# Fourteen expert units started beside the last batches' routing, in a fused attention and mixture-of-experts kernel

## Chip, cores and metric

One core of one Trainium2 chip. The metric is the device time of one execution in microseconds (us). The engines are TensorE (PE; PEld are its weight loads), VectorE (DVE), ScalarE (ACT), GpSimd (POOL) and SyncE (SP), which mostly issues DMAs.

## The reference, cut to what matters

```python
S, D, heads of 64, E, R, K = 512, 512, 8, 8, 128, 2        # x, ctx_1024: (8, 512, 512) float32
# attention of x over ctx_1024, per batch and head
q, k, v = layernorm(x) @ Wq, ctx @ Wk, ctx @ Wv
x = x + tanh(g_xattn[0]) * (softmax(q k^T / 8) v @ Wo + bo)
# mixture of experts, on all 4096 tokens
z = layernorm(x)
topv, topi = top_k(z @ gate_w, 2);  w = softmax(topv)
u, v = z @ Wu[e], z @ Wv[e]                                 # e: each token's two experts
x = x + tanh(g_ffn[0]) * sum over the two of  w * (silu(u) * v) @ Wo[e]
```

The router gives each of the 4096 tokens two of eight experts, so the eight lists hold 8192 entries in all, of sizes that depend on the data.

## The kernel before, in words

**Attention.** Batches b = 0 to 7 have four steps j each, so g = 4b + j runs from 0 to 31. A step handles two heads: their scores, the softmax and its product with V, and beside it the projections of q and k for two heads to come, and work on the next batch's tokens. Numbers are carried as a float16 high part and a low part, with three products (PASSES) for one. An exponential needs the row maximum first: `row_max_scores` makes an approximate score block per head h and tile t on PE (L1275), 8 a step, `row_max` reduces it on DVE (L873), and `max_transpose` (L1280) turns the result. PE's order is written out by hand in `step`.

**Second norm and routing.** A step g of batch b also finishes a 128-token tile n = g - 4 of the batch before: transposes of the heads' output into oT (`transposes`, L1242), `out_project` (12 products of 128x512, L1233), `x2_rows` on DVE, store of the new x to the output. Then come `factors2`, `normalise2` and `row_lo`, which make the normed row's two halves, `turn` (a DMA transpose) and `logits`. After four tiles `best_two`, `ranks`, `take_ranks` and `places` give each token its place in the two lists, and `scatter` on POOL writes its row (2064 bytes) there with 8 indirect DMAs for a batch (L576). The ring of rows has 6 slots. All the G products of attention and routing take turns in two PSUM banks, in the order that `bank_uses` lists.

**Tail.** Batch 7's tiles have no later step, so a loop over g = 32 to 37 does them alone. It also makes the logits and places of batch 6. `unit_table` on DVE then lists the units: a unit is a window of UR = 256 rows of one expert's list, and there are UNITS = 32 + 7 = 39 of them, of which the ones beyond the real blocks repeat rows of the last list with weight 0.

**Units.** SP loads a unit's 256 rows (516 KB, 6 slots ahead), PE turns them (L1449), multiplies by the expert's weights (L1457, L1468), ACT scales (L830), and POOL adds the two tiles of results onto the output with two indirect accumulating DMAs (L662). Two units may name the same token. So `unit(s)` always waits until unit s - 2's adds have landed, and where the expert changes or two windows of one list overlap also for those of unit s - 1. That is what `need` says:

```python
if 0 < s < 3:
    pool.wait_ge(added[(s - 1) % 2], 2 * 16)
if s >= 3:
    before = pool.value_load(need[0:1, s:s + 1], min_val=2 * 16, max_val=32 * UNITS)
    pool.wait_ge(added[(s - 1) % 2], before)
```

Within a list the last block goes first, then the others from the start. ACT writes results into a ring of 4, so it waits for the adds of unit s - 4.

## Time and profile before

| | us |
|---|---|
| median of 3 runs | 1108.74 |
| their range | 1103.36 to 1109.86 |
| the profiled execution | 1095.86 |
| its span, first to last instruction | 1094.1 |

The span is what the trace shows; 1.76 us lie around it. The profiled execution is one run, and faster than the three timed ones. A view's start times are counted from the span's start, L numbers are lines of the kernel before, and in brackets behind a row stands how long the engine was idle before it and what ended that.

### The profile page before, as it was taken

The numbers are of one execution on the slowest core, as the hardware profiler recorded it, in microseconds if no ns is written. First come the engines' busy times: TensorE is split into PE (matmuls) and PEld (weight loads), VectorE is DVE, ScalarE is ACT, GpSimd is POOL, SyncE is SP. The second block draws the span as 40 slices with busy tenths as digits, with TensorE's granted clock in tenths as the row PEclk, the third lists the DMA queues.
The fourth block names the chain that finished last, engine by engine and source line by source line (L and its number), as shares of the span: only waits on it lengthen the run. The fifth ranks groups of instructions, "written<-read, shape, count | busy, mean of one in ns | idle before, by whom it ended". The sixth has DMA issues, their size and how long they took to land.

```text
span 1094.1 us, 22759 instructions
## 1 busy us (share of the span) xinstructions
PE 902.0 (82%) x8210; PEld 546.8 (50%) x8210; DVE 677.7 (62%) x1595; ACT 570.5 (52%) x1022; POOL 536.3 (49%) x645
## 2 busy tenths in 40 slices
PE   4888878998899899899899989886650899799890
PEld 2344435555455455455555545443320777677660
DVE  5687757777777767767777776586234454344440
ACT  4366646566556656556655656456210465555450
POOL 6122324253465366447546543645563146666564
PEclk9999989999999999999999999998665899999995
DMA  8555773422362264254336228334343588999996
GB/s 274 154 161 158 236 244 78 141 73 74 97 199 71 65 199 112 60 177 112 76 88 208 67 63 266 95 93 146 97 142 105 151 195 170 181 195 194 185 159 81
DMA packets 125325, 154.26 MB, mean 141 GB/s; under 512 B 48288, under 2 KB 81056, under 8 KB 124832
## 3 DMA queue, kind: packets, MB, share of 16 engines
q1 hardware_dynamic: 108352, 115.40, 36.0%
q0 software_dynamic: 16864, 37.40, 17.8%
q8 instruction: 69, 1.13, 0.4%
q14 instruction: 40, 0.33, 0.1%
HBM read 62.83 MB, written 56.30 MB: 109 GB/s over the span
## 4 chain that ended last, share of the span: by engine, by line
PE 51%; DVE 12%; DMA 11%; issue 9%; ACT 7%; POOL 6%; SPq 2%; POOLq 1%; ACTq 0%; DVEq 0%
PE G L1233 26%; DMA out_dram<-V,Ph 7%; PE MX L1275 4%; PE ST L1290 3%; PE ST L1289 3%; PE MX L1457 3%; PE G L1242 3%; POOL out_dram L662 2%; PE PV L1302 2%; PE PV L1304 2%; PE PV L1306 2%; DVE tiles L863 2%; DVE mx L873 2%; POOL expert_rows L576 2%; PE G L1449 1%
## 5 line engine op out<-in xcount | busy, mean ns | idle before, releaser
L619 POOL TENSOR_TENSOR Pl<-P,Ph 128x512 f16<-128x512 f32 x128 | 150.6, 1184 | 223.5 <-ACT Ph L697 223.0
L694 ACT ACTIVATE P<-ST 128x512 f32<-128x512 f32 x256 | 153.3, 599 | 203.3 <-PE ST L1290 194.4
L873 DVE TENSOR_REDUCE mx<-MX 128x1 f32<-128x512 f32 x256 | 168.1, 684 | 26.4 <-PE MX L1275 26.4
L697 ACT ACTIVATE Ph<-ST 128x512 f16<-128x512 f32 x256 | 154.6, 604 | 0.4
L662 POOL DMA_INDIRECT out_dram<-V,Ph x78 | 122.5, 1571 | 48.1 <-ACT V L830 28.4
L1457 PE MATMUL MX<-heads,tiles 128*128 128x256 f16 x936 | 119.8, 280 | 16.5 <-DVE heads L1187 16.3
L1302 PE MATMUL PV<-V,Ph 128*128 128x65 f16 x1024 | 114.2, 196 | 23.0 <-issue 23.0
L1302 PEld LDWEIGHTS PV<-V,Ph 128*128 128x128 f16 x1024 | 97.9, 98 | 43.8 <-issue 26.2
L1304 PE MATMUL PV<-V,Ph 128*128 128x64 f16 x1024 | 114.5, 197 | 0.0
L1306 PE MATMUL PV<-V,Pl 128*128 128x65 f16 x1024 | 114.1, 195 | 0.0
L1457 PEld LDWEIGHTS MX<-heads,tiles 128*128 x936 | 91.5, 100 | 38.6 <-issue 21.3
L1304 PEld LDWEIGHTS PV<-V,Ph 128*128 128x128 f16 x1024 | 97.4, 99 | 18.6 <-issue 1.1
L1289 PE MATMUL ST<-heads 128*128 128x512 f16 x256 | 98.6, 385 | 6.7 <-DMA heads<-mrow 3.8
L1290 PE MATMUL ST<-heads 128*128 128x512 f16 x256 | 98.8, 386 | 0.0
L1306 PEld LDWEIGHTS PV<-V,Pl 128*128 128x128 f16 x1024 | 97.8, 101 | 0.0
L911 DVE TENSOR_TENSOR Pl<-P,Ph 128x512 f16<-128x512 f32 x128 | 95.9, 751 | 2.5 <-ACT Ph L697 2.5
L1275 PE MATMUL MX<-heads 128*128 128x512 f16 x256 | 89.2, 384 | 9.4 <-DVE mx L873 9.2
L1233 PE MATMUL G<-tiles,wq_hi 128*128 128x512 f16 x256 | 79.0, 391 | 12.9 <-DVE tiles L863 12.9
L1233 PE MATMUL G<-wv_hi,tiles 128*128 128x512 f16 x256 | 81.7, 379 | 0.0
L563 POOL TENSOR_TENSOR second_norm<-second_norm,tgbo 128x512 f32<-128x512 f32 x32 | 42.5, 1328 | 74.1 <-DMA second_norm<-in_x_dram 73.8
L1233 PE MATMUL G<-tiles,wk_hi 128*128 128x512 f16 x256 | 76.2, 379 | 0.2 <-DVE k_lo L863 0.2
L918 DVE SCALAR_TENSOR_TENSOR second_norm<-G,gate,second_norm 128x512 f32<-128x512 f32 x32 | 24.0, 750 | 84.0 <-PE G L1233 78.1
(206 smaller groups left out, 1917.6 us busy)
## 6 DMA issues: line engine op xcount, KB each, us to landing
heads<-expert_rows SPq DMA_DIRECT2D x39, 516.0 KB, 5.5
tiles<-in_x_dram SPq DMA_DIRECT2D x32, 256.0 KB, 4.8
tiles<-in_ctx_dram SPq DMA_DIRECT2D x32, 256.0 KB, 5.2
second_norm<-in_x_dram SPq DMA_DIRECT2D x32, 256.0 KB, 3.2
out_dram<-second_norm SPq DMA_DIRECT2D x32, 256.0 KB, 2.4
heads<-q_hi SPq DMA_DIRECT2D x124, 64.0 KB, 2.0
heads<-k_hi SPq DMA_DIRECT2D x124, 64.0 KB, 2.0
expert_rows<-second_norm SPq DMA_DIRECT2D x2, 2064.0 KB, 11.0
```

What stands on the lines that cost most here:

```text
L619: nc.gpsimd.tensor_tensor(Pl[:, hh, c, :], P32[:, c, :], Ph[:, hh, c, :], ALU.subtract).then_inc(pl_pool, 1)
L662: nc.gpsimd.indirect_dma_start(out_rows, bass.IndirectOffsetOnAxis(ids[:, s, k:k + 1], 0), y_sb[:, s % YR, k, :], None, compute_op=ALU.add) \
L694: nc.scalar.activation(P32[:, c, :], ST[:, c % 2, :], ACT.Exp, scale=0.125 / SC2).then_inc(p_ready, 1)
L697: nc.scalar.activation(Ph[:, hh, c, :], ST[:, c % 2, :], ACT.Exp, scale=0.125 / SC2).then_inc(ph_ready, 1)
L873: nc.vector.tensor_reduce(out=mx[:, k // TT, k % TT:k % TT + 1], in_=MX[:, (k + odd) % 2, :], axis=AXX, op=ALU.max).then_inc(mx_taken, 1)
L1233: last = nc.tensor.matmul(out_, a, m, start=(n == 0), stop=(n == len(parts) - 1))
L1275: nc.tensor.matmul(MX[:, (k + g) % 2, :], Q1[:, s, h, t * P:(t + 1) * P], K1[:, s, h, :], start=True, stop=True).then_inc(mx_filled, 1)
L1290: nc.tensor.matmul(ST[:, c % 2, :], K2[:, j, hh, cols], Q2[:, j, hh, :], start=False, stop=True).then_inc(st_filled, 1)
L1302: nc.tensor.matmul(out_[:, 0:HD + 1], Ph[:, hh, c, cols], V[:, r, c, h, 0:HD + 1], start=(c == 0), stop=False)
L1304: nc.tensor.matmul(out_[:, 0:HD], Ph[:, hh, c, cols], V[:, r, c, h, HD + 1:], start=False, stop=False)
L1306: last = nc.tensor.matmul(out_[:, 0:HD + 1], Pl[:, hh, c, cols], V[:, r, c, h, 0:HD + 1], start=False, stop=(c == TT - 1))
L1457: last = nc.tensor.matmul(dst, w, uT[:, s % 2, a, c * UR:(c + 1) * UR], start=k == 0, stop=k == len(parts) - 1)
```

## The change

1. **Early units.** After step 30, when batches 0 to 5 have their places, `early_table` (DVE, some 32 small instructions) picks EARLY = 14 units among blocks that are full already. It takes level by level, one block from the end of each list's full blocks, then a second one of the first lists that have it, and lists them by expert. `unit_table` is cut into `unit_experts`, `unit_windows` and `unit_needs` for the LATE = 25 other units, which skip the blocks taken.
2. **Interleaving.** The tail loop is gone. Its work stands in gaps v = 0 to 10 (GAPS = 11) of the unit loop on every engine, by `tail_uses`, `between`, `ahead_of` and `late_in`. The G banks are then shared by units and tail: each side waits for the other's evacuations. SP requests the rows of the first six units when the scores are done and batches 0 to 5 are scattered, and from unit 14 on waits for the late table and all scatters.
3. **Buffers.** Batch 7's residuals are loaded at once into the idle O buffer (`x2_of`), its rows go into the wq and wk buffers (`row_of`), and the early table lies in xn.
4. **Output waits.** Adds of units 0 to 13 wait only for the stores of batches 0 to 5; unit 14 for all stores and for unit 13's adds. In the late list a change of expert needs no wait when one window lies wholly below, the other wholly above `cut`, each list's length after batch 4.
5. **Row maxima.** `row_max_scores` contracts over 64 rows instead of 128: head 0 of a pair from partitions 0 to 63, head 1 from 64 to 127, each into its own MX bank, and the two follow one another on PE.

Cut to its core; `late=True` in PE's `between` is the place behind the v products:

```diff
+def tail_uses(v, first, late):
+    if late:
+        return [("out", first + v)] if v <= 3 else [("ranks", first // 4)] if v == 8 else []
+    names = [("oT", first + v)] if v <= 3 else []
+    if v in (0, 2):
+        names.append(("logits", first - 2 + v // 2))
+    if v == 4:
+        names.append(("ranks", first // 4 - 1))
+    if 4 <= v <= 7:
+        names.append(("logits", first + v - 4))
+    return names
...
+            def between(v):
+                n = TILES - TT + v
+                if v == 0:
+                    turn(n - 1)
+                if 1 <= v <= 4:
+                    store_x2(n - 1)
+                if 2 <= v <= 5:
+                    turn(n - 2)
+            load_last_residuals()
+            sp.wait_ge(early_ready, 3)
+            sp.wait_ge(st_filled, STEPS * 8)
+            for r in range(2):
+                for h in range(2):
+                    sp.wait_ge(scattered[r][h], EARLY_BATCHES // 2 * 2 * K * 16)
+            for s in range(XG):
+                unit_rows(s)
             for s in range(UNITS):
-                unit_rows(s)
+                if s < GAPS:
+                    between(s)
+                if s + XG == EARLY:
+                    sp.wait_ge(table_ready, 2)
+                    sp.wait_ge(outsider_st, E * K * 16)
+                    for r in range(2):
+                        for h in range(2):
+                            sp.wait_ge(scattered[r][h], B // 2 * 2 * K * 16)
+                if s + XG < UNITS:
+                    unit_rows(s + XG)
             for r in range(2):
...
+            def between(v):
+                n = TILES - TT + v
+                if v == 0:
+                    factors2(n - 1)
+                    add_bias(n)
+                    row_lo(n - 1)
+                    for t in range(1, TT):
+                        add_bias(n + t)
+                if 1 <= v <= 4:
+                    factors2(n - 1)
+                if v in (5, 9):
+                    scatter(B - 2 + v // 9, 0)
+                    scatter(B - 2 + v // 9, 1)
+            def unit_add(s):
                 pool.wait_ge(ids_ready, s + 1)
-                if 0 < s < 3:
-                    pool.wait_ge(added[(s - 1) % 2], 2 * 16)
-                if s >= 3:
-                    before = pool.value_load(need[0:1, s:s + 1], min_val=2 * 16, max_val=32 * UNITS)
-                    pool.wait_ge(added[(s - 1) % 2], before)
+                if s in (0, EARLY):
+                    for r in range(2):
+                        pool.wait_ge(x2_st[r], (EARLY_BATCHES * TT if s == 0 else TILES) // 2 * 16)
+                if s and (s < 3 or s == EARLY):
+                    pool.wait_ge(added[(s - 1) % 2], ((s - 1) // 2 + 1) * 2 * 16)
+                elif s:
+                    wanted = pool.value_load(listed(e_need, l_need, s)[0:1], min_val=2 * 16, max_val=32 * UNITS)
+                    pool.wait_ge(added[(s - 1) % 2], wanted)
...
-            for s in range(UNITS):
-                unit(s)
+            pool.wait_ge(early_ready, 3)
+            for v in range(UNITS + 2):
+                if v < GAPS:
+                    between(v)
+                if v == EARLY + 1:
+                    pool.wait_ge(table_ready, 3)
+                if v >= 2:
+                    unit_add(v - 2)
+                if 1 <= v <= 4:
+                    row_lo(TILES - TT + v - 1)
...
+                nc.vector.tensor_tensor(above, limit, cut_u, ALU.is_ge)
+                nc.vector.tensor_tensor(flag[:, ahead], off[:, here], off[:, ahead], ALU.subtract)
+                link(nc.vector.scalar_tensor_tensor(out=below, in0=limit, scalar=float(UR), in1=cut_u,
+                                                    op0=ALU.add, op1=ALU.is_le))
+                nc.vector.tensor_tensor(done[:, ahead], below[:, ahead], above[:, here], ALU.mult)
+                link(nc.vector.tensor_tensor(blocks[:, ahead], above[:, ahead], below[:, here], ALU.mult))
+                nc.vector.tensor_tensor(first_[:, ahead], l_ue[:, here], l_ue[:, ahead], ALU.not_equal)
+                link(nc.vector.tensor_tensor(done[:, ahead], done[:, ahead], blocks[:, ahead], ALU.max))
+                nc.vector.tensor_scalar(blocks[:, ahead], flag[:, ahead], float(-UR), None, ALU.is_gt)
+                link(nc.vector.tensor_tensor(first_[:, ahead], first_[:, ahead], done[:, ahead], ALU.is_gt))
+                link(nc.vector.scalar_tensor_tensor(out=flag[:, ahead], in0=flag[:, ahead], scalar=float(UR),
+                                                    in1=blocks[:, ahead], op0=ALU.is_lt, op1=ALU.mult))
+                link(nc.vector.tensor_tensor(flag[:, ahead], flag[:, ahead], first_[:, ahead], ALU.max))
+                nc.vector.scalar_tensor_tensor(out=l_need[:, here], in0=flag[:, ahead], scalar=32.0,
+                                               in1=C["need"][:, EARLY:UNITS - 1],
+                                               op0=ALU.mult, op1=ALU.add).then_inc(table_ready, 1)
...
+                link(nc.vector.tensor_scalar(below_all, level_sum, float(EARLY), None, ALU.is_le))
+                link(nc.vector.tensor_reduce(level, below_all, AXX, ALU.add))
+                nc.vector.tensor_tensor(e_cum[:, 0, :], full, level.to_broadcast([P, E]), ALU.is_gt)
+                link(nc.vector.tensor_tensor(used, full, level.to_broadcast([P, E]), ALU.min))
+                link(nc.vector.tensor_reduce(spare_sum, used, AXX, ALU.add))
+                link(nc.vector.tensor_scalar(spare_sum, spare_sum, -1.0, float(EARLY), ALU.mult, ALU.add))
...
             def row_max_scores(g, k):
                 s, turn = slot_and_use(g)
-                h, t = k // TT, k % TT
+                t, h = divmod(k, 2)
+                rows_ = slice(h * HD, (h + 1) * HD)
                 if k == 0:
                     pe.wait_ge(qk_dma[s], turn * QK_DMAS * 16)
                 if k == 1:
                     since(pe, mrow_ready, g)
                 else:
                     since(pe, mx_taken, g * (2 * TT) + k - (1 if k > 1 else 0))
-                nc.tensor.matmul(MX[:, (k + g) % 2, :], Q1[:, s, h, t * P:(t + 1) * P], K1[:, s, h, :],
+                nc.tensor.matmul(MX[:, h, :], Q1[rows_, s, h, t * P:(t + 1) * P], K1[rows_, s, h, :],
                                  start=True, stop=True).then_inc(mx_filled, 1)
...
                     n = "qk"[k // 2]
                     scores(b, j, k)
-                    maxima(2 * k)
+                    maxima(2 * k, 2 * k + 1)
                     if proj and k % 2 == 0:
                         dst = bank((n, g))
                         if j == 2 and k == 0:
                             pe.wait_ge(evacuated, use[n, g])
                         product(dst, parts[n], 0, 6)
-                    maxima(2 * k + 1)
...
-            pe.wait_ge(table_ready, 1)
-            pe.wait_ge(evacuated, len(uses))
+                return pe.value_load(listed(e_expert, l_expert, s)[0:1], min_val=0, max_val=E - 1)
+            pe.wait_ge(early_ready, 1)
             unit_transposes(0)
             for n in "uvo":
                 pe.wait_ge(fw_back[n], 16)
             e = expert_of(0)
             for s in range(UNITS):
+                if s < GAPS:
+                    between(s, False)
                 pe.wait_ge(t_hi, s + 1)
                 pe.wait_ge(t_lo, s + 1)
                 since(pe, a_done, s)
...
                     unit_transposes(s + 1)
                 since(pe, s_done, s)
                 up("v", Vp, e, s, v_filled)
+                if s < GAPS:
+                    between(s, True)
                 if s:
                     down(s - 1, e_before)
                 e_before = e
+                if s == EARLY - 1:
+                    pe.wait_ge(table_ready, 1)
                 if s < UNITS - 1:
                     e = expert_of(s + 1)
             down(UNITS - 1, e_before)
```

## Rows read from the trace of the kernel before

**Rows 1.** The page: busy time of each engine
```profile
PE 902.0 (82%) x8210; PEld 546.8 (50%) x8210; DVE 677.7 (62%) x1595; ACT 570.5 (52%) x1022; POOL 536.3 (49%) x645
```

**Rows 2.** Stretches: busy (count) of PE, PEld, DVE, ACT, POOL; PEclk, DMA share, GB/s
```profile
260.00:660.00 400.00, 365.75 (x3500) 208.65 (x3498) 295.85 (x665) 238.64 (x443) 215.68 (x275) 0.99 0.41 112
780.00:785.00 5.00, 3.50 (x10) 1.17 (x9) 0.69 (x1) 2.00 (x3) 1.15 (x1) 0.50 0.04 8
...
865.00:965.00 100.00, 93.11 (x872) 73.24 (x870) 48.41 (x170) 54.63 (x93) 57.36 (x50) 0.98 0.87 182
```

**Rows 3.** Timeline where attention ends and where units began: start, length, engine, line
```profile
772.76 0.96 POOL L576 DMA_INDIRECT expert_rows<-second_norm,pos_staged  x1 [0.30 <-issue]
...
842.08 0.96 POOL L576 DMA_INDIRECT expert_rows<-second_norm,pos_staged  x1 [0.30 <-issue]
...
846.15 2.65 SPq L522 DMA_DIRECT2D heads<-expert_rows  x3
...
849.86 1.44 PE L1449 MATMUL G<-identity,heads 128*128 128x128 f16 x12 [20.16 <-DMA heads<-expert_rows]
```

**Rows 4.** POOL's timeline: adds of results (L662), two a unit
```profile
865.16 1.61 POOL L662 DMA_INDIRECT out_dram<-V,Ph  x1 [12.17 <-ACT V L830]
...
893.19 1.56 POOL L662 DMA_INDIRECT out_dram<-V,Ph  x1 [3.07 <-ACT V L830]
895.05 1.57 POOL L662 DMA_INDIRECT out_dram<-V,Ph  x1 [0.30 <-issue]
900.77 0.19 POOL L543 TENSOR_TENSOR junk<-ones 128x1 f32<-128x1 f32 x1 [4.15 <-DMA out_dram<-V,Ph]
901.46 1.56 POOL L662 DMA_INDIRECT out_dram<-V,Ph  x1 [0.50 <-issue]
...
905.27 1.56 POOL L662 DMA_INDIRECT out_dram<-V,Ph  x1 [0.16 <-POOL junk L543]
...
1082.02 1.56 POOL L662 DMA_INDIRECT out_dram<-V,Ph  x1 [0.44 <-issue]
```

**Rows 5.** PE's timeline: row transposes of two units in a row
```profile
889.23 1.06 PE L1449 MATMUL G<-identity,heads 128*128 128x128 f16 x16
...
894.04 1.06 PE L1449 MATMUL G<-identity,heads 128*128 128x128 f16 x16
```

**Rows 6.** The table of waits in the unit stage: us, times, longest
```profile
POOL junk L543 <- DMA out_dram<-V,Ph: 43.7, 8, 6.8
```

**Rows 7.** PE's timeline in attention: two row-maximum products in a row
```profile
395.20 0.59 PE L1275 MATMUL MX<-heads 128*128 128x512 f16 x2
```

**Rows 8.** PE's timeline: transposes to score product, without and with the small transpose
```profile
338.44 0.63 PE L1242 MATMUL G<-identity,tiles 128*128 128x128 f32 x4 [0.77 <-DVE oT_lo L863]
338.90 0.38 PE L1289 MATMUL ST<-heads 128*128 128x512 f16 x1
...
403.63 0.63 PE L1242 MATMUL G<-identity,O 128*128 128x128 f32 x4 [0.30 <-DVE k_lo L863]
404.10 0.27 PE L1280 MATMUL MX<-identity,mneg 128*8 128x128 f32 x1
404.20 0.38 PE L1289 MATMUL ST<-heads 128*128 128x512 f16 x1
```

**Rows 9.** Timelines of POOL (residual, scatters) and of DVE (unit table)
```profile
763.01 1.26 POOL L563 TENSOR_TENSOR second_norm<-second_norm,tgbo 128x512 f32<-128x512 f32 x1 [5.38 <-DMA second_norm<-in_x_dram]
...
803.02 0.19 POOL L543 TENSOR_TENSOR junk<-ones 128x1 f32<-128x1 f32 x1
...
812.47 0.96 POOL L576 DMA_INDIRECT expert_rows<-second_norm,pos_staged  x1 [0.30 <-issue]
...
831.85 0.16 DVE L1011 TENSOR_TENSOR nt<-base,list_starts 128x8 f32<-128x8 f32 x1
...
841.57 0.20 DVE L1055 SCALAR_TENSOR_TENSOR Ph<-Ph,adds_before 128x38 uint32<-128x38 f32 x1
```

**Rows 10.** PE's waits in attention: us, times, longest
```profile
PE G L1242 <- DVE oT_lo L863: 15.0, 9, 2.4
```

More of the change, by code:

```diff
@@ new lines, in layer @@
+        l_ids = take(K * LATE).bitcast(U32).rearrange("p (u k) -> p u k", k=K)
+        valid = take(K * LATE).rearrange("p (u k) -> p u k", k=K)
+        spare_n = xn[:].rearrange("p k d -> p (k d)")
+        at = Count()
+        take = lambda n: spare_n[:, at.take(n):at.value]
+        e_ue, e_expert, e_off, e_need = (take(EARLY) if k == 0 else take(EARLY).bitcast(U32) for k in range(4))
+        e_uw = take(4 * EARLY).rearrange("p (k u) -> p k u", k=4)
+        levels = take(EB * E).rearrange("p (l e) -> p l e", l=EB)
@@ new lines, in layer, with listed @@
+        level_sum, below_all, level, spare_sum = take(EB), take(EB), take(1), take(1)
+        e_ids = take(K * EARLY).bitcast(U32).rearrange("p (u k) -> p u k", k=K)
+        e_cmp = take(E * BE).rearrange("p (e b) -> p e b", e=E)
+        e_ucmp, e_ucmp2 = (take(EARLY * E).rearrange("p (u e) -> p u e", e=E) for _ in range(2))
+        e_cum = take(4 * E).rearrange("p (k e) -> p k e", k=4)
+        full, low, cut = take(E), take(E), take(E)
+        used = take(E)
+        def listed(early, late, s):
+            return early[:, s:s + 1] if s < EARLY else late[:, s - EARLY:s - EARLY + 1]
@@ L1004, in outsiders, with running_sum, unit_experts @@
                 nc.vector.tensor_tensor(out_pos[:], before, spare_place, ALU.add).then_inc(outsider_ready, 1)
-            def unit_table():
-                spread_e = lambda z: z.unsqueeze(1).to_broadcast([P, UNITS, E])
-                spread_u = lambda z: z.unsqueeze(2).to_broadcast([P, UNITS, E])
-                before, block_, limit, off, over, blocks, flag = (uw[:, k, :] for k in range(7))
+            def running_sum(z):
+                for k, d in enumerate((1, 2, 4)):
+                    nc.vector.tensor_copy(z[:, k + 1, 0:d], z[:, k, 0:d])
+                    link(nc.vector.tensor_tensor(z[:, k + 1, d:E], z[:, k, d:E], z[:, k, 0:E - d], ALU.add))
+            spread_e = lambda z: z.unsqueeze(1).to_broadcast([P, LATE, E])
+            spread_u = lambda z: z.unsqueeze(2).to_broadcast([P, LATE, E])
+            first_, j_, limit, off, start_, blocks, flag, done, cut_u, below, above, over = (uw[:, k, :] for k in range(12))
+            def unit_experts():
+                number = C["unit_no"][:, 0:LATE]
+                nc.vector.tensor_tensor(low, full, used, ALU.subtract)
                 link(nc.vector.tensor_tensor(nt[:, 0, :], base[:], C["start"][:], ALU.subtract))
@@ L1433, in _, with between, ahead_of_turn @@
             pe.wait_ge(o_ready, B * HB)
-            for g in range(STEPS, STEPS + 6):
-                if g < STEPS + 4:
-                    transposes(("oT", g - 4), O[(B - 1) % 2][:, g - STEPS, :])
-                    out_project(g - 4)
-                logits(g - 6)
-                if g % 4 == 1:
-                    ranks(g // 4 - 2)
+            def between(v, late):
+                for name in tail_uses(v, TILES - TT, late):
+                    what, n = name
+                    if what == "out":
+                        out_project(n)
+                    elif what == "oT":
+                        transposes(name, O[(B - 1) % 2][:, v, :])
+                    elif what == "logits":
+                        logits(n)
+                    else:
+                        ranks(n)
+            def ahead_of_turn(s):
+                names = [n for v in range(min(s, GAPS)) for late in (False, True)
+                         for n in tail_uses(v, TILES - TT, late) if not (late and v == s - 1)]
+                return 1 + max(use[n] for n in names) if names else use["oT", TILES - TT]
             def unit_transposes(s):
                 r = s % XG
+                units_turned.take()
                 pe.wait_ge(rows_ld[r], (s // XG + 1) * 16)
+                pe.wait_ge(evacuated, ahead_of_turn(s))
                 for a, taken in ((0, t_hi), (1, t_lo)):
```

321 lines of the change are left out of this document (189 added, 132 removed).

## The prediction

> **What bounds the kernel now.** I read the page's busy shares first, then a table by stage, then the waits and the timelines. TensorE (PE) is busy for 82% of the span [rows 1], but the stages differ [rows 2]. In attention (260 to 660 us) PE is busy 91% of the time at a clock share of 0.99, with DVE at 74%. From 780 us, when the last head is done, to 850 us, PE almost stops: that is the routing of the last batches, a chain of small steps through every engine. Then come 39 units. Their first 256 rows are requested at 846.15, PE turns them at 849.86, and the first add of a result is issued at 865.16 [rows 3, 4]. The last unit's add is issued at 1082.02 [rows 4], 12.1 us before the span ends at 1094.1.
>
> In the unit stage the queue that sets the pace is GpSimd's (POOL's). A PE unit takes 4.81 us when nothing holds it (889.23 to 894.04) [rows 5], so 38 intervals would be 183 us. The adds take 216.9. The reader should see two kinds of interval in their timeline. A free one is 3.81 us (901.46 to 905.27): two issues and a small POOL instruction. A held one waits until the adds of the unit before have landed: 895.05 + 1.57 ends the issue, 4.15 us of wait follow, and the next add starts at 901.46, 8.27 us after 893.19 [rows 4]. So a held interval is 4.12 us plus its wait. The table of waits has 8 such waits of 43.7 us together, 5.46 on average and 6.8 at the longest [rows 6]: 9.6 us on average, 10.9 at most.
>
> I worked out the routing from the reference's inputs. The eight lists have 1147, 971, 688, 1113, 1074, 929, 1219 and 1051 tokens, 36 blocks. Units 1 and 2 always wait. Each of the 7 changes of expert holds, and so does the first of the 3 spare units: 10 held intervals, which is two more than the 8 of the table (the first two end with ACT). Counted alike the held ones take 10 x 9.6 = 96 us, and the 28 others (216.9 - 96)/28 = 4.3 on average.
>
> **The change, part by part.**
>
> (a) The units' start moves. The last scatter of batch 5 is issued at 772.76 [rows 3]. Before, the last scatter of all, at 842.08, was followed by the request for rows 4.07 us later; the same step gives 776.8, and with 3.7 us to landing 780.5, more with six requests together: 782.5. Before, first transposes to first add took 15.3 us [rows 3, 4]. Now PE also has, ahead of unit 0's down product, two blocks of oT transposes (0.63 each), two output projections of 12 matmuls at a pitch of 0.21 us, 2.5 us each [rows 7, 8], and their evacuations, much of it at the half clock (0.50 at 780 to 785, 1.2 GHz) [rows 2]: about +10 us. First add: 782.5 + 25.5 = 808 instead of 865.2, **57 us earlier**.
>
> (b) The adds wait more often. Early units go one level at a time, so experts change often. Batches 0 to 5 give 3, 2, 1, 3, 3, 2, 3, 3 full blocks; 14 units are 2, 2, 1, 2, 2, 2, 2, 1 of them. Held are units 1, 2, 4, 5, 7, 9, 11, 13, and 14 by a fixed wait. Of the 22 real late units the rule on token ranges releases only some: a list's last low block beside the next list's end. But lists 0, 3, 4, 6 and 7 have a further block above the early ones, and that one comes last, so ten transitions stay held, plus the first spare unit. Together **20 held and 18 free intervals instead of 10 and 28**. Nothing else on POOL hides them, as the same queue issues every add.
>
> (c) The last batches' routing goes beside units 0 to 10. PE then needs about 10 us a unit in the first two intervals: 4.8 + 2.5 + 0.6, and the shared G banks make each piece wait for the evacuation of the last. On POOL, ahead of adds 3 and 7, stand eight scatters, 803.02 to 813.43, 10.4 us [rows 9]; with the issues of the add before them (3.4) and a start of 0.5 an interval is 14.3, and the landing of the add before is hidden under them. The residual additions, the row splits and the factors lie in the waits of held adds. The unit table, 831.85 to 841.57 [rows 9] on an idle PE before, is cut into three pieces beside units 8 to 10; its some 60 instructions cost nothing as long as POOL is behind, and up to 10 us if it is not. Unit 14's rows wait for scatter 7; PE reaches them at about the same time: 0 to 3 us, I take 0.
>
> (d) The sum. Which price has a held interval? The DMA engines were 0.87 busy from 865 to 965 us [rows 2]; the same bytes, spread over some 50 us more, load them less. Between 8.3 and 9.6 I take 8.9. A free one is POOL's own pace more often now, between 3.81 and 4.3: 3.9. Two intervals at 10, two at 14.3, seventeen held at 8.9 = 151.3, seventeen free at 3.9 = 66.3: 266.2 us against 216.9, **49.3 us more**. First add 57 earlier, chain 49 longer: **8 us gained**. With 8.3 and 3.8 it is 20; with 9.6 and 4.3 it is 11 us lost.
>
> (e) The early table, some 32 small DVE instructions, stands between steps 30 and 31: 7 us by the pace of the old table (39 in 9.9). Step 31 was held by POOL, which waited 5.38 us for a residual until 763.01 [rows 9], so most is covered: 0 to 7, I take **2 lost**.
>
> (f) The row-maximum products now use 64 rows each, the two heads of a pair in the two halves of the array, side by side, in fixed banks. Before, two in a row are recorded with 0.59 us and one product of that width with 0.38 [rows 7, 8], a pitch of 0.21 us each. If the halves run together a pair saves 0.15 to 0.2; 4 pairs in 31 steps are 124 pairs, 19 to 25 us of PE. Does it reach the end? PE is 91% busy in attention, its waits there are on DVE and ACT hand-overs, such as 15.0 us on oT_lo [rows 10], and these would grow; I count 0.65: **12 us gained**. If they run one after the other it is 0. The odd products also move ahead of half a projection, which gives DVE its maxima earlier; but PE's largest wait is another one; taken as 0.
>
> What does a change of the array's shape cost? The trace has one: the transpose of the maxima uses 8 columns, on a 32-column tile. With it, four transposes to the next score product take 0.57 us (403.63 to 404.20); without it 0.46 (338.44 to 338.90) [rows 8]. The difference, 0.11, is the small transpose itself, so two changes of shape cost next to nothing. The Trainium skill, "TensorEngine Tiling (Array Packing)", Key Properties, says that tiles can execute matmuls in parallel, but that changing the tiling mode drains TensorE. By that drain the sum would turn: that is rival 2. The row is of a change in columns, not in rows, so it doesn't settle it.
>
> In all: 1095.86 - 8 + 2 - 12 = 1078, by the profiled execution, which had 1.76 us around its span. It was 12.9 us faster than the median shown, 1108.74; scaled, the forecast is **1091 us**, 1.6% faster. A measurement of this kernel can hardly tell under 1% from no change.
>
> **Rivals.**
>
> 1. The adds' queue eats it all (slower). The long waits for landing stay at 9.6 us and free intervals at 4.3: (d) loses 11, (e) 2, and (f) brings nothing because DVE and ACT hold PE: 1109, scaled 1122. It decides from a held interval of 9.35 us, where at 3.9 for the free ones the 57 us are used up. For it: the number of held intervals doubles. Against it: the load falls.
>
> 2. The halves drain the array. A 512-column product is recorded for 0.38 us at a pitch of 0.21 [rows 7, 8], so a drain could show 0.16 at each side of a pair: 0.33 lost, 0.15 won, 22 us over 124 pairs, of which I count 18. With the 8 and the 2: 1108, scaled 1121. For it only the page; against it the trace's one change of shape [rows 8].
>
> 3. The halves don't overlap and cost nothing, everything else as forecast: 1090, scaled 1103, within 1%.
>
> 4. Better than forecast: landings fall to 4.15 us of wait and PE keeps all it wins: 1095.86 - 20 + 1 - 20 = 1057, scaled 1070.
>
> **How the numbers follow.** Forecast (the case of 1082 to 1098) 0.38, rival 4 (1062 to 1082) 0.18, rival 3 (1098 to 1110) 0.20, rival 1 0.12, rival 2 0.12. Faster by over 1% (under 1097.7) is the first two, with a little of rival 3: 0.58. Slower by over 1% (over 1119.8) is half of the last two and a tail: 0.14. The rest, 0.28, is within 1%. The range of 8 in 10 reaches from 1066 to 1120.
>
> **What would show it.** (a) The first add at 805 to 812. (b) 20 intervals of 8 to 10 us, nine of them up to add 14. (c) Two gaps of about 14 us with the scatters in them. (d) Last add at about 1062 to 1068, if attention is shorter by 10 to 12 us. (f) Pairs of 64-row products that start less than 0.1 us apart, and a product after them no later than 0.3 us from the first; and attention's last head 8 to 15 us earlier. Wrong it would be if held intervals cost over 9.4, if the pairs are 0.4 us or longer, or if the first four units go at over 12 us each because of the G banks and the half clock; each us there is 4 on the first adds.

## The result, and the profile after

The kernel before: 1106.21 us (median of 7 runs, 1100.50 to 1109.86). The changed kernel: 1113.46 us (7 runs). The ratio is 1.0085, 95% interval 1.0051 to 1.0119. It is taken from the changed kernel's six runs that were not slow by chance (the seventh took 1121.42); the quotient of the two medians shown is 1.0066. The changed kernel is slower by a little under 1%, where 1.6% faster had been forecast. The time lies in the range of 1066 to 1120, but above 1110, where only rivals 1 and 2 stood, with 0.12 each. The profiled execution of after took 1118.5 us, its span 1116.8.

The busy line of its page answers to [rows 1]:

```profile
PE 913.6 (82%) x8210; PEld 533.8 (48%) x8210; DVE 686.0 (61%) x1648; ACT 570.2 (51%) x1022; POOL 537.8 (48%) x645
```

The stretches of after, as in [rows 2]:

```profile
260.00:660.00 400.00, 361.72 (x3446) 196.08 (x3445) 295.51 (x659) 235.02 (x437) 216.54 (x273) 0.99 0.41 111
...
800.00:850.00 50.00, 40.86 (x342) 28.35 (x341) 24.22 (x87) 21.15 (x35) 21.57 (x32) 0.89 0.50 115
850.00:900.00 50.00, 33.58 (x290) 24.47 (x288) 24.72 (x121) 15.32 (x26) 32.36 (x35) 0.84 0.80 198
```

PE is busy for the same share as before. The idle stretch of [rows 2] at 780 us is gone, but at 850 to 900 us, where units were to run at full pace, PE is idle a third of the time. The hand-over, from the timelines of SP, PE and POOL in after, answers to [rows 3, 4]; the last row is the last unit's first add:

```profile
787.48 2.91 SPq L566 DMA_DIRECT2D heads<-expert_rows  x3
...
791.66 1.65 PE L1644 MATMUL G<-identity,heads 128*128 128x128 f16 x14 [4.68 <-DMA heads<-expert_rows]
...
817.00 1.67 POOL L734 DMA_INDIRECT out_dram<-V,xn  x1 [0.41 <-issue]
...
1104.35 1.56 POOL L734 DMA_INDIRECT out_dram<-V,Ph  x1 [0.58 <-issue]
```

The adds began at 817.0 instead of 865.2 and ended at 1104.4 instead of 1082.0. Their chain took 287.4 us instead of 216.9. The table of waits of after in the unit stage, us, times and longest, answers to [rows 6]:

```profile
POOL junk L612 <- DMA out_dram<-V,Ph: 55.8, 11, 7.2
...
POOL junk L612 <- DMA out_dram<-V,xn: 32.5, 6, 6.5
```

17 waits of 88 us stand where 8 of 44 stood, 5.2 us each on average instead of 5.5. To see where the time went, I cut the span at three landmarks that both traces have: DVE's last copy of row maxima in attention (745.34 before, 752.06 after), the first add, and the last. The last column is a second trace of the changed kernel (e8, below):

| stretch | before | forecast | after | after again |
|---|---|---|---|---|
| start to the last row maxima | 745.3 | -12 | +6.7 | -0.4 |
| from there to the first add | 119.8 | -55 | -54.9 | -55.2 |
| first to last add | 216.9 | +49.3 | +70.5 | +65.5 |
| behind the last add | 12.1 | 0 | +0.4 | +0.2 |
| span | 1094.1 | -18 | +22.7 | +10.1 |

The second line is the forecast to 0.2 us. The first is 12 to 19 us off, and since it differs by 7 us between two traces of one kernel, it is no row to build on alone. The third is 16 to 21 us off.

### The profile page after: what moved, and what is told of

Read it like the earlier page. It is cut to its first block, busy times and chain, and to the rows that moved or that the text cites. A ratio compares the mean times of both kernels' runs of the same rounds, so it can differ in the third digit from the quotient of the medians.

```text
span 1116.8 us, 22814 instructions
## 1 busy us (share of the span) xinstructions
PE 913.6 (82%) x8210; PEld 533.8 (48%) x8210; DVE 686.0 (61%) x1648; ACT 570.2 (51%) x1022; POOL 537.8 (48%) x645
## 4 chain that ended last, share of the span: by engine, by line
PE 54%; DMA 12%; issue 10%; DVE 9%; ACT 8%; POOL 3%; SPq 2%; POOLq 0%; ACTq 0%; DVEq 0%
PE G L1416 27%; DMA out_dram<-V,Ph 8%; PE MX L1652 4%; PE ST L1473 4%; PE ST L1474 4%; PE G L1425 3%; PE MX L1459 3%; POOL out_dram L734 2%; PE PV L1490 2%; PE PV L1486 2%; PE PV L1488 2%; DVE tiles L942 2%; PE G L1644 2%; ACT V L902 1%; DMA out_dram<-V,xn 1%
## 5 line engine op out<-in xcount | busy, mean ns | idle before, releaser
L952 DVE TENSOR_REDUCE mx<-MX 128x1 f32<-128x512 f32 x256 | 163.1, 680 | 25.2 <-PE MX L1459 24.4
L1652 PE MATMUL MX<-heads,tiles 128*128 128x256 f16 x936 | 130.4, 294 | 42.7 <-DVE heads L1356 35.9
L1652 PEld LDWEIGHTS MX<-heads,tiles 128*128 x936 | 94.7, 105 | 70.2 <-issue 51.8
L1473 PE MATMUL ST<-heads 128*128 128x512 f16 x256 | 98.9, 386 | 12.1 <-ACT Ph L777 9.5
L734 POOL DMA_INDIRECT out_dram<-V,Ph x50 | 77.9, 1557 | 23.7 <-ACT V L902 12.8
L634 POOL TENSOR_TENSOR second_norm<-second_norm,tgbo 128x512 f32<-128x512 f32 x28 | 36.9, 1319 | 69.8 <-DMA second_norm<-in_x_dram 69.7
L612 POOL TENSOR_TENSOR junk<-ones 128x1 f32<-128x1 f32 x56 | 27.3, 488 | 88.7 <-DMA out_dram<-V,Ph 55.8
L997 DVE SCALAR_TENSOR_TENSOR second_norm<-G,gate,second_norm 128x512 f32<-128x512 f32 x28 | 21.0, 750 | 77.0 <-PE G L1416 52.0
```

The lines of the kernel that those rows point to most:

```text
L734: nc.gpsimd.indirect_dma_start(out_rows, bass.IndirectOffsetOnAxis(ids_of(s)[:, k:k + 1], 0), y_sb[:, s % YR, k, :], None, compute_op=ALU. ...
L952: nc.vector.tensor_reduce(out=mx[:, k % 2, k // 2:k // 2 + 1], in_=MX[:, k % 2, :], axis=AXX, op=ALU.max).then_inc(mx_taken, 1)
L1473: nc.tensor.matmul(ST[:, c % 2, :], K1[:, j, hh, cols], Q1[:, j, hh, :], start=True, stop=False)
L1652: last = nc.tensor.matmul(dst, w, uT[:, s % 2, a, c * UR:(c + 1) * UR], start=k == 0, stop=k == len(parts) - 1)
```

## The experiments

Times are medians, ratios are to the kernel before on the same chip at the same time. That kernel itself had medians from 1095.5 to 1106.4 us in the four sessions, so only ratios are compared across them. L numbers in a row are lines of its own run's kernel.

**The row maxima: e1, e2, e3, e12.** e1 is the kernel before with the whole of part 5. e2, and e12 once more, have its order alone; e3 has its shape alone:

```diff
 e1, e3 (shape)
-nc.tensor.matmul(MX[:, (k + g) % 2, :], Q1[:, s, h, t * P:(t + 1) * P], K1[:, s, h, :],
+nc.tensor.matmul(MX[:, h, :], Q1[rows_, s, h, t * P:(t + 1) * P], K1[rows_, s, h, :],
 e1, e2, e12 (order)
-                    maxima(2 * k)
+                    maxima(2 * k, 2 * k + 1)
...
-                    maxima(2 * k + 1)
```

> The kernel before with part 5 of the change alone (64-row row-maximum products in pairs). In the trace of after the last copy of row maxima in attention comes 6.7 us later than before. Theory S (shape): entering and leaving the 64-row shape costs 0.10 and 0.11 us at each pair, which is what the overlap wins (0.22), and the first products of a pair no longer start ahead of what they wait for; so this part alone loses 5 to 8 us, 1112 to 1114 against 1106, ratio 1.005 to 1.007. Rival G (the forecast): the part gains 12 us and something else of the change lengthened attention: ratio 0.989. Rival N: it does nothing: ratio 1.000, and the 6.7 us belong to the other parts.

> The kernel before with only the order of part 5: the two row-maximum products of a pair follow one another on PE, ahead of half a projection, but contract over 128 rows and alternate banks as before. Theory S: the shape is what costs, so this is within 1.5 us of the kernel before, ratio 0.999 to 1.001. Rival O (order): the second product of a pair now waits for DVE's reduction of the product before the last, which half a projection used to cover; then this kernel carries the whole loss, +5 to +8 us, ratio 1.005 to 1.007.

> The kernel before with only the shape of part 5: 64-row products in fixed banks, but each at its old place, so that no two of them run together and each is entered and left by itself. Theory S: eight excursions a step at 0.10 + 0.11 us and no overlap, 248 of them, 52 us of PE, of which some two thirds reach the end: +34 us, 1140, ratio 1.03 (1.02 to 1.045). Rival O: the shape costs nothing in itself and only the order does: ratio 1.000.

> e2 once more (kernel before, the two row-maximum products of a pair in a row). If its 0.4% was real: ratio 0.994 to 0.998. If it was chance: 0.998 to 1.002.

Measured: e1 1096.51, ratio 0.9988 (0.9951 to 1.0024). e2 1091.90, 0.9959 (0.9921 to 0.9996). e12 1093.24, 0.9971 (0.9953 to 0.9989). e3 1115.62, 1.0168 (1.0124 to 1.0212).

Theory S had the mechanism and missed the size: the shape costs in e3, but e1 as a whole comes to nothing, and the 6.7 us longer attention of the first trace of after did not belong to part 5. Two executions with the attention code of before (e5 and e7, below) had it 8.3 and 10.6 us longer than the trace of before. Rival N holds for e1. e2 lies below both of its expectations. The timelines of PE and of its weight loads show why the pair gains nothing. First e1: the pair, with its weight load (PEld), between the second score product ahead of it and the projection behind it:

```profile
395.06 0.38 PE L1291 MATMUL ST<-heads 128*128 128x512 f16 x1
395.37 0.10 PEld L1276 LDWEIGHTS MX<-heads 64*128 64x128 f16 x2 [0.42 <-issue]
395.38 0.39 PE L1276 MATMUL MX<-heads 64*128 64x512 f16 x2
395.70 0.60 PE L1233 MATMUL G<-tiles,wq_hi 128*128 128x512 f16 x2
```

The same place in e2, with 128 rows:

```profile
394.30 0.38 PE L1290 MATMUL ST<-heads 128*128 128x512 f16 x1
394.31 0.31 PEld L1275 LDWEIGHTS MX<-heads 128*128 128x128 f16 x2
394.52 0.59 PE L1275 MATMUL MX<-heads 128*128 128x512 f16 x2
394.95 0.59 PE L1233 MATMUL G<-tiles,wq_hi 128*128 128x512 f16 x2
```

And a single 64-row product in e3:

```profile
400.78 0.38 PE L1291 MATMUL ST<-heads 128*128 128x512 f16 x1
401.09 0.39 PE L1276 MATMUL MX<-heads 64*128 64x512 f16 x1
401.41 0.61 PE L1233 MATMUL G<-tiles,wq_hi 128*128 128x512 f16 x2
```

The reader should compare starts. In e1 two products of 64 rows are recorded as 0.39 us together, so the halves do run side by side. But the pair begins 0.32 us behind the product ahead and the next one 0.32 behind it, where the pitch is 0.22 and 0.21: 0.64 us in all. In e2 it is 0.65. What the overlap wins (0.21) goes at the two changes of shape. The 126 pairs of each trace that stand between 512-column products agree: 0.63 us in e1 and 0.65 in e2, at the median. The weight loads show something more. In e2 a load starts 0.21 us ahead of its product (394.31 and 394.52), under the product before it. In e1 it starts together with its product (395.37 and 395.38), and it lasts 0.10 us, which is what a change of shape costs. Whether the load that is no longer hidden is the cause, or only shows the pause, no run here settles.

In e3 a 64-row product that stands alone takes 0.63 from the product ahead to the one behind, where two pitches of 0.22 (0.43) would do: 0.20 lost. But the expectation counted too many of them. In the old order half of the pairs have nothing between their two products ([rows 7] is one), and these still run together in e3, at 0.63. Its trace has 120 row-maximum products that stand alone, not 248: 24 us of PE. The time rose by 18 us (1.68% of 1095.5; 14 to 23 by the confidence interval). So I estimate that a microsecond of PE in attention is worth some 0.8 at the end (0.6 to 1.0), and the 0.65 that I had taken was not the error. The Trainium skill, "TensorEngine Tiling (Array Packing)", Key Properties, had both halves of this: tiles work in parallel, a change of mode drains. It gives no price; these rows do, some 0.10 us at each side. That what costs it is a drain is the page's word, not the trace's.

The order alone gains 0.3 to 0.4% in both runs. I had taken it as 0; why it gains was not tried. e1 has this order too, so its 64-row shape and fixed banks may lose as much again. The intervals of e1 and e2 overlap, so that is not shown.

**The rest without the row maxima: e4, and after again: e8.** e4 has parts 1 to 4 and the row maxima of before; e8 is the changed kernel.

> The changed kernel with the row maxima of before (parts 1 to 4 alone). Theory S: attention is 6.7 us shorter than in the changed kernel and the rest is the same, 1106 to 1107, ratio to the kernel before 1.000 to 1.002: the units' earlier start is used up by the adds' chain exactly. Rival G: the 64-row products gain 12 us and this kernel is slower than the changed one, 1125, ratio 1.017. Rival O with nothing of the shape gives the same as S here.

> The changed kernel itself once more, beside the two below and on their chip, with a profile. By e1 the 64-row row maxima change nothing, and by e4 the rest costs 1.0%: ratio to the kernel before 1.008 to 1.010. In the trace: first add 63 to 66 us after the last copy of row maxima, a chain of adds of 284 to 288 us, of it 78 to 79 in the first seven intervals.

Measured: e4 1109.38, ratio 1.0103 (1.0067 to 1.0139). e8 1107.66, 1.0112 (1.0076 to 1.0149). Parts 1 to 4 alone cost the 1%. Rival G is out; so is S's size, which had left nothing to them. Since the stretch before the first add is as forecast, all that is wrong with the sum but (f) must then lie in the chain of adds: 283.6 us in e4 and 282.4 in e8 (1.6 under what was expected of e8), against 219.4 to 221.1 in e1, e2, e3 and e12.

**How much of it are held intervals: e5, e6, e7.** e5 and e6 leave out the waits on unit s - 1 and the tokens' own rows: the adds go to rows that no neighbour has, so their output is not the reference's. They show times alone:

```diff
-nc.vector.tensor_copy(ids[:, s, :], column(0)).then_inc(ids_ready, 1)
+nc.vector.tensor_scalar(ids[:, s, :], C["row_no"][:], 12.0, float(s % 12), ALU.mult, ALU.add).then_inc(ids_ready, 1)
...
-pool.wait_ge(added[(s - 1) % 2], before)
```

> The kernel before, with adds that never name a row of the unit before: each unit's 256 results are added to rows 12r + (s mod 12) of the output, spread over the first 3072 rows, and the waits on unit s - 1 are gone (that on unit s - 2 stays). The results thus go to wrong rows. Theory H (held intervals set the chain): 38 intervals at PE's own cadence of 4.81 us = 183 instead of 217 us, so 34 us less, 1072, ratio 0.97. Rival M (the DMA engines set it: 0.87 busy between 865 and 965 us): with the waits gone the landing takes longer and the wait on unit s - 2 takes their place, a chain of 205 or more, ratio 0.99.

> The changed kernel, with adds to rows of their own and no wait on unit s - 1, as in e5. Theory H: 36 intervals of 4.81 and two with eight scatters in them (14.3): 202 us instead of 287, the last add at about 1019, some 85 us less than the changed kernel if PE in the gaps keeps up with 10 us for the first four intervals: up to 16 us of that is lost again. 1030 to 1050, ratio to the kernel before 0.93 to 0.95. Rival R (the routing's work in the gaps is itself what takes the time): the first eleven intervals stay as long as they are (106 us together) and only the later ones shrink: 106 + 27 x 4.81 = 236, 51 us less than the changed kernel, 1062, ratio 0.96.

e7 adds ten waits to the kernel before:

```diff
+if s in (4, 7, 14, 19, 20, 24, 28, 29, 33, 34):
+    pool.wait_ge(added[(s - 1) % 2], ((s - 1) // 2 + 1) * 2 * 16)
```

> The kernel before with ten more waits for the landing of unit s - 1, at adds 4, 7, 14, 19, 20, 24, 28, 29, 33 and 34, so that 20 intervals are held as in the changed kernel, and everything else is as it was. Theory H: each turns an interval of 4.3 into one of 9.3: +50 us, 1156, ratio 1.045. With the forecast's price (8.9 and 3.9, and the others catching up): +39, ratio 1.035. Rival M: the landings get shorter as the engines are less busy and the free intervals between catch up: +25 us or less, ratio 1.02.

Measured: e5 1068.37, ratio 0.9666 (0.9616 to 0.9717). e6 1060.81, 0.9578 (0.9527 to 0.9629). e7 1136.55, 1.0262 (1.0206 to 1.0317). The chains, from POOL's timelines, as intervals from one unit's first add to the next one's:

```
                    chain   intervals 1-7   intervals 8-38   held in 8-38
before              216.9        45.9           171.0             7
e5 before, free     183.3        34.5           148.8             0
after               287.4        78.9           208.5            15
e8 after again      282.4        77.4           205.0            15
e6 after, free      227.9        79.0           148.9             0
```

The table answers in two parts. In intervals 8 to 38 theory H holds: without holds both kernels run at 4.80 us a unit, with PE busy for the whole of the window in e5:

```profile
875.00:975.00 100.00, 100.00 (x954) 79.45 (x951) 54.79 (x189) 61.88 (x104) 71.07 (x63) 1.00 1.02 218
```

A hold there costs (171.0 - 148.8)/7 = 3.2 us before and (205.0 - 148.9)/15 = 3.7 after; in e7, (251.3 - 183.3)/20 = 3.4. That is less than the difference between a held and a free interval, since PE works ahead meanwhile: in e7 the 20 held intervals take 9.04 and the 18 free ones 3.91, under the 4.8 of e5, where the results come just ahead of the adds. e7's expectation was too high for this reason: 29 us for ten holds (23 to 35 by the confidence interval), nearest to rival M's 25. But the sum of intervals 1 to 7 does not fall when the holds go: 79.0 without, 77.4 and 78.9 with them. There rival R is right. The single intervals do change. In e6 interval 4 is 3.8 instead of 9.6, and interval 7 is 19.0 instead of 14.4, because POOL then waits 4.82 us for DVE's places before the second set of scatters.

So of the 65.5 us by which the chain of e8 is longer than that of before, 31.5 lie in the first seven intervals, and by e6 the routing sets these (no run took the routing away and kept the holds); 34 are the eight more holds behind them.

**What the first seven are made of: e9, e10.** POOL's timeline in after, from the first add of unit 2 to the two of unit 3 (five scatters from 849.68 to 855.82, like those shown, and one small operation are left out):

```profile
841.01 1.66 POOL L734 DMA_INDIRECT out_dram<-V,xn  x1 [0.39 <-issue]
842.96 1.58 POOL L734 DMA_INDIRECT out_dram<-V,xn  x1 [0.30 <-issue]
846.53 1.15 POOL L638 TENSOR_TENSOR wk_lo<-second_norm,wk_lo 128x512 f16<-128x512 f32 x1 [1.99 <-ACT wk_lo L811]
848.00 0.19 POOL L612 TENSOR_TENSOR junk<-ones 128x1 f32<-128x1 f32 x1 [0.32 <-DVE pos_staged L1068]
848.35 1.03 POOL L647 DMA_INDIRECT expert_rows<-second_norm,pos_staged  x1 [0.16 <-issue]
...
856.13 1.03 POOL L647 DMA_INDIRECT expert_rows<-second_norm,pos_staged  x1 [0.30 <-issue]
857.47 0.96 POOL L647 DMA_INDIRECT expert_rows<-second_norm,pos_staged  x1 [0.30 <-issue]
858.46 0.20 POOL L612 TENSOR_TENSOR junk<-ones 128x1 f32<-128x1 f32 x1
858.82 1.59 POOL L734 DMA_INDIRECT out_dram<-V,xn  x1 [0.16 <-issue]
```

Interval 3 is 17.8 us: two issues, a row split that waits for ACT, eight scatters of 1.27 each, and behind them unit 3's add, whose result had been there. Add 3 waits for no landing, so nothing hides the scatters. e9 is e4 with the scatters in halves ahead of adds that do wait for one:

```diff
-                if v in (5, 9):
-                    scatter(B - 2 + v // 9, 0)
-                    scatter(B - 2 + v // 9, 1)
+                if v in (6, 7, 9, 11):
+                    scatter(B - 2 + v // 9, v in (7, 11))
```

> The kernel of e4 (changed kernel, row maxima of before) with the eight scatters of each of the last two batches cut in halves of four, each half in the queue right ahead of an add that waits for a landing anyway: ahead of adds 4, 5, 7 and 9 in place of all eight ahead of adds 3 and 7. Theory Q (GpSimd's queue is what the first intervals are made of, and a landing of 5.5 us hides the 5.2 us of four scatters): interval 3 falls from 17 to 8 or 9, interval 7 from 14 to 10, the rest is the same: 11 to 13 us less than e4, about 1097, ratio to the kernel before 0.998 to 1.000. Rival P (TensorE's extra work in the gaps sets the first intervals, the scatters lie beside it): the adds 4, 5 and 9 come later by what add 3 gains: 0 to 3 us less, ratio 1.008 to 1.010.

> e9 with the order of e2 as well (the two row-maximum products of a pair in a row, 128 rows as before). If the 0.4% of e2 holds: 4 us less than e9, ratio to the kernel before 0.994 to 0.996 under theory Q, 1.004 to 1.006 under rival P; if e2's gain was chance, the same as e9.

Measured: e9 1097.16, ratio 1.0009 (0.9985 to 1.0033). e10 1094.17, 0.9974 (0.9945 to 1.0004). Theory Q holds: 0.93% less than e4, 10 us, where it said 11 to 13. In e9's trace the first seven intervals take 65.6 us instead of 78.0; interval 3 is 7.1, interval 7 is 9.1. POOL in e9 between the adds of units 3 and 4 (two scatters left out):

```profile
841.75 1.55 POOL L731 DMA_INDIRECT out_dram<-V,xn  x1 [0.30 <-issue]
842.76 0.76 POOL L612 TENSOR_TENSOR junk<-ones 128x1 f32<-128x1 f32 x1
843.68 1.02 POOL L647 DMA_INDIRECT expert_rows<-second_norm,pos_staged  x1 [0.16 <-POOL junk L612]
...
847.72 0.96 POOL L647 DMA_INDIRECT expert_rows<-second_norm,pos_staged  x1 [0.31 <-issue]
851.17 0.19 POOL L612 TENSOR_TENSOR junk<-ones 128x1 f32<-128x1 f32 x1 [2.48 <-DMA out_dram<-V,xn]
851.87 1.60 POOL L731 DMA_INDIRECT out_dram<-V,xn  x1 [0.51 <-issue]
```

The scatters end at 848.7 and the landing is waited for until 851.2, so POOL loses no time by them. The landing itself may come later beside them: interval 4 is 12.0 us in e9 and 9.7 in e4, interval 5 is 10.5 and 10.8. The order of e2 gives its 0.35% again, though the confidence intervals of e9 and e10 overlap.

**Fewer holds: e11.** e10 with EARLY = 11, the last four scatters ahead of add 8 instead of 9, `unit_needs` one gap earlier, and in late lists of four or more units the last two swapped (`j_` is the unit's place in its list, `blocks` the list's late units):

```diff
-    EARLY = 14
+    EARLY = 11
...
+link(nc.vector.tensor_tensor(cut_u, j_, blocks, ALU.subtract))
+nc.vector.tensor_scalar(below, cut_u, -3.0, None, ALU.is_equal)
+link(nc.vector.tensor_scalar(above, cut_u, -2.0, None, ALU.is_equal))
+nc.vector.tensor_scalar(cut_u, blocks, 3.5, None, ALU.is_gt)
+link(nc.vector.tensor_tensor(below, below, above, ALU.subtract))
+link(nc.vector.tensor_tensor(below, below, cut_u, ALU.mult))
+link(nc.vector.tensor_tensor(j_, j_, below, ALU.add))
```

> e10 with EARLY = 11 in place of 14 and, in late lists of four or more units, the last two swapped, so that a list ends with a block below the cut and the change to the next list's last block needs no wait. By the routing 16 intervals are held (1, 2, 4, 5, 7 to 11, 14 to 18, 21, 28) in place of 20; the last scatters stand ahead of adds 7 and 8. Theory H: four holds less at 9.3 - 4.4 = 4.9 us each, 20 us less than e10: chain 251, 1075, ratio to the kernel before 0.980. Rival T (the late table and the last scatters now hold TensorE before unit 11, as unit 14's rows held it for 7.2 us in e9): that wait grows to 12 to 20 us and takes the place of the four holds: 0 to 8 us less than e10, ratio 0.990 to 0.997.

Measured: 1082.03, ratio 0.9890 (0.9856 to 0.9923). It is the fastest kernel here that leaves nothing out, 1.1% faster than before and some 2% than the changed one. It lies between theory and rival, just outside rival T's 0.990, which its interval takes in. The chain fell from 270.9 to 258.5, not 251. I see two reasons, and this one run doesn't part them. At 3.4 us a hold (e7), four are worth 14 us, not 20. And rival T came true in part: PE waited long for the rows of unit 11, which stand behind the last scatters, and interval 9 grew to 15.3 us, 6 more than a held one. The row of PE's timeline in e11:

```profile
886.86 1.89 PE L1649 MATMUL G<-identity,heads 128*128 128x128 f16 x16 [19.38 <-DMA heads<-expert_rows]
```

## Why the prediction was wrong, point by point

**(a) Start of the units, (e) early table: right.** From the last row maxima to the first add 64.9 and 64.6 us; the forecast was 119.8 - 57 + 2 = 64.8. The sign that I had named, a first add at 805 to 812, came in e8 (809.5) and not in the first trace (817.0), which had the longer attention.

**(b) Number of holds: right.** POOL's intervals show 20 held ones, among them the nine that were named up to add 14, and eleven behind them as counted. Interval 3 is long too, by the scatters.

**(c) The first intervals: mis-sized.** With the prices of (c) and (d), intervals 1 to 7 come to 10 + 10 + 14.3 + 8.9 + 8.9 + 3.9 + 14.3 = 70.3 us; measured 78.9 and 77.4. Intervals 1 and 7 were as forecast (9.8; 14.5 and 14.4). Missed were 3 to 4 us in interval 2 and 3.5 in interval 3. Adds stand behind row splits (and the next tile's factors, 1.9 us) in POOL's queue, and these wait for ACT, which waits for the tile's chain through PE, DVE and POOL. I had put the row splits "in the waits of held adds", but adds 1 and 2 wait longer for their split than they would for a landing (their results had lain ready for 4.9 us), and add 3 waits for none. The sign for this had been named, first four units at over 12 us each, and it came: 13.1 on average, 12.5 in e8. It had no term in the sum. The unit table cost nothing, as forecast: in e9 the last routing work of DVE ends at 883.8 us, before the adds reach unit 9.

**(d) Price of the intervals: mis-sized; the free ones left out a wait.** In e8 the 15 held intervals from 8 on average 9.05 us (8.9 forecast) and the 16 free ones 4.33 (3.9): 2 and 7 us. In the first trace it is 9.30 and 4.31, 6 and 7 us, so the held ones came near the 9.4 that would have shown me wrong. I had taken 3.9 because POOL would always be the late one. That is so in the first free interval behind a hold: the nine of e8 take 3.80 to 3.88. The seven that follow another free one take 3.8 to 7.0, 5.0 on average, and what they wait for stood in no term of mine: the wait for unit s - 2, which every add has. The timelines of ACT and POOL in e8: unit 23's results, the first add of unit 21, its landing (ACT waits for it too, to reuse the place of these results), and unit 23's add:

```profile
981.66 1.26 ACT L902 ACTIVATE V<-PV,unit_scales 128x512 f32<-128x512 f32 x2 [6.33 <-DMA out_dram<-V,Ph]
...
990.63 1.56 POOL L734 DMA_INDIRECT out_dram<-V,Ph  x1 [0.50 <-ACT V L902]
...
999.92 1.27 ACT L902 ACTIVATE V<-PV,unit_scales 128x512 f32<-128x512 f32 x2 [6.61 <-DMA out_dram<-V,Ph]
1000.60 1.56 POOL L734 DMA_INDIRECT out_dram<-V,Ph  x1 [2.51 <-ACT V L902]
```

The last row names ACT as what ended the wait, but unit 23's results had been there since 982.9. The landing of unit 21 had not: it came at 999.9, and the add stands 0.7 us behind it. In the traces of e8 and e4 each of the six free intervals over 4.0 us from 8 on ends 0.75 us behind such a landing, with its own results ready 12 to 18 us before. So both kinds of interval hang on the landing, in e8 8.3 us behind a unit's first add on average (7.1 to 10.3). A held one is that and 0.75, 9.0. A second free one is what is left of it, 8.3 + 0.75 - 3.8 = 5.2. I had taken the wait on unit s - 2 as never late.

PE is not on this path, though it does stop when ACT has no free place and then starts again at the lower clock. PE's timeline and a window of e8, in a row of five holds:

```profile
966.56 2.74 PE L1652 MATMUL MX<-heads,tiles 128*128 128x256 f16 x12 [3.30 <-DVE heads L1356]
...
976.97 1.47 PE L1652 MATMUL MX<-heads,tiles 128*128 128x256 f16 x12
```

```profile
966.60:969.00 2.40, 2.40 (x12) 1.71 (x13) 1.00 (x6) 0.42 (x1) 1.26 (x1) 0.50 0.98 163
```

Twelve products take 2.74 us at a clock share of 0.50 (1.2 GHz), after 3.3 us of idle time, and 1.47 at full clock. No add from 8 on waited for that.

In e7 only three of the 18 free intervals follow another free one. There they do cost 3.91 and held ones 9.04: my two prices were right for that pattern, and the pattern here is another.

**(f) Row maxima: the step that failed as a mechanism.** 12 us were forecast, 0 came (e1). The overlap is real, 0.21 us a pair, as is a cost at each side as in rival 2 (0.10 us instead of its 0.16), and they cancel. I had let the trace's one change of shape stand for all [rows 8] in the sum, though I had said that it doesn't settle it. That was a change in columns, and its product is small. The sign that I had named, a product behind the pair no later than 0.3 us from the pair's start, looked at one side only: that distance is 0.32, and 0.32 more lie ahead of the pair. The weight of a microsecond was not the error: by e3's some 0.8, nearer the 18 of 22 that I had given to rival 2 than the 0.65 here, a real gain would have been worth 15 to 19 us.

**The reasons added up.** Two steps failed: (f), which counted the overlap and took the changes of shape as free, and the chain of adds in (c) and (d), sized 16 to 21 us too short, which had no term for the row splits ahead of the first adds nor for the wait on unit s - 2. Of the difference between forecast and e8 in the span, 28 us, (f) is 12 and the chain 16: 7 of it in intervals 1 to 7, 9 in 8 to 38. By its terms rival 1 came closest: "adds' queue eats it all" with 9.6 and 4.3, a chain of 285 us, and nothing from (f). It had 0.12. That its 285 fits is in part luck: its held intervals at 9.6 were too dear by 0.3 to 0.6 us each, and that stood in for what it, too, had left out of the first seven. Its scaled time of 1122 was too slow, as was rival 2's 1121. Its reason for (f), that DVE and ACT hold PE, was not the one. Rival 3 said 1103 and is refuted in its reason: the halves do overlap.

**The reference point.** I summed against one execution that had been 12.9 us faster than the median. Its chain of adds, 216.9, is also the shortest of five with that tail. The others took 219.4 to 221.1, which moves the sum by 3 to 4 us in the change's favour and so was not the error. A second trace of the changed kernel was worth more than any reading of the first: the 6.7 us of attention were gone in it.

**What stays open.** Why attention took 8 to 11 us longer in some executions of the same code was not tried. The long ones (752.1 in the first trace of after, 753.7 to 756.0 in e5, e6 and e7) lie in the two sessions in which the kernel before had a median of 1106 us. The other traces had 740.9 to 747.8, but for e3 with its shape. Nor was what ends the long wait at 856 to 863 us in after, where PE, ACT and DVE stand idle together; e4 and e8 have no such stop and nearly the same chain.

## What to carry to other kernels

Work that is moved beside a serial queue is only free inside that queue's waits: find the waits that end on something else (a landing) and put it there, in pieces of the wait's length. It was 10 us here (e9 against e4), for the same work. Before starting work earlier, count what the new order adds to the last queue: 55 us of earlier start were less than 8 to 10 more serialised adds and the routing between them. And price a change of array shape at both sides of each excursion, not by another kind of change. A timeline can name the wrong releaser of a wait: check when the one that it names had been done (here the results had lain ready for 17 us). Last, count in an experiment's trace how often it did what it was built for: e3 set 120 products apart, not 248.

## What the runs showed of the hardware

- Two 512-column products of 64 rows in the two halves of the array run as one (0.39 us recorded for both, e1). Entering and leaving that shape from 128-row products costs 0.10 us each at full clock: a single pair breaks even with two 128-row products (0.64 against 0.65), a lone 64-row product loses 0.20 (e3). Behind a change the weight load starts with its product, and not 0.21 us ahead of it as between products of one shape.
- With adds that never wait for their neighbour's landing, PE ran 100% busy at full clock with a DMA share of 1.02 (e5), 4.8 us a unit, the pace of [rows 5]. POOL's queue, which can go at 3.8, does not set the pace without holds. The DMA engines were as full as PE, so whether they would have let a faster PE through is not shown.
- One hold lengthens the chain by 3.2 to 3.7 us (before, e7, e8), though its interval is some 5 us longer than a free one. A unit's adds have landed 7.1 to 10.3 us behind the first of them (e8, from unit 7 on), and a wait even for the last unit but one shows: two free intervals in a row take at least that landing and 0.75 us.
